# Routing the first chunks of a mixture-of-experts kernel earlier, and moving shared work and tables between its stages

## The reference

```python
scores = sigmoid(x @ gate_w.T)
choice = scores + gate_bias            # 8 groups of 8 experts
group_scores = sum(top_k(choice.reshape(T, 8, 8), 2)[0], -1)
# keep the 4 best groups, set the rest of choice to 0, take the 8 best experts
w = scores[chosen] / (sum(scores[chosen]) + 1e-20) * 2.5
out = sum over experts of w * down(silu(x @ gate.T) * (x @ up.T)) + shared(x)
```

## Time and profile before

| | |
|---|---|
| Runs shown | 659.68 us median of 3 (657.02 to 660.19) |
| The profiled execution | 659.67 us, of which the span of instructions is 657.9 us |
| Busy: PE, DVE, POOL, ACT | 588.1, 461.0, 444.8, 325.7 us |
| Granted TensorE clock, mean | 0.966 of full speed |

### The profile page before, as it was taken

The page is one execution under the profiler, slowest core; times in us unless marked ns, Lnnn a source line. Parts: engine busy times, 40 slices in busy tenths (PEclk is TensorE's granted clock), DMA queues, the critical chain, the costliest instruction groups (busy, mean ns, idle before and its releaser), DMA issues.

```text
span 657.9 us, 13016 instructions
## 1 busy us (share of the span) xinstructions
PE 588.1 (89%) x3456; PEld 472.5 (72%) x3457; DVE 461.0 (70%) x1311; ACT 325.7 (50%) x637; POOL 444.8 (68%) x464
## 2 busy tenths in 40 slices
PE   2986988888889899999996999999999999999980
PEld 2655666665655899999994999999995666666640
DVE  3446688888756789767773567677475598868785
ACT  8474866665553454555552455555552135252332
POOL 1003777777777777777776777777764777777773
PEclk9988899998997999999998999999999999999995
DMA  8962666661112678777755688888866223222122
GB/s 211 383 133 52 138 156 144 148 141 53 53 49 84 179 230 237 230 227 224 230 159 141 184 235 228 242 232 234 228 198 203 53 53 95 56 69 65 52 65 64
DMA packets 124609, 101.35 MB, mean 154 GB/s; under 512 B 15334, under 2 KB 114494, under 8 KB 124094
## 3 DMA queue, kind: packets, MB, share of 16 engines
q1 hardware_dynamic: 63766, 48.41, 27.9%
q0 software_dynamic: 14336, 29.39, 15.3%
q10 hardware_dynamic: 46464, 23.07, 12.1%
HBM read 52.58 MB, written 48.23 MB: 153 GB/s over the span
## 4 chain that ended last, share of the span: by engine, by line
PE 41%; POOL 31%; issue 12%; DVE 5%; DMA 4%; ACT 3%; SPq 1%; POOLq 0%; DVEq 0%; ACTq 0%
POOL xs_dram L513 29%; PE GU L820 8%; PE OT L840 6%; PE GU L880 4%; PE GU L881 4%; PE XT L889 4%; PE HT L829 3%; PE XT L809 3%; DMA arena<-os_dram,gslots 2%; POOL arena L518 2%; PE GU L601 1%; PE GU L752 1%; PE GU L751 1%; DMA xs_dram<-x1r,slots 1%; SPq L444 1%
## 5 line engine op out<-in xcount | busy, mean ns | idle before, releaser
L513 POOL DMA_INDIRECT xs_dram<-x1r,slots x224 | 225.7, 1007 | 123.5 <-issue 67.5
L518 POOL DMA_INDIRECT arena<-os_dram,gslots x224 | 217.0, 969 | 80.6 <-issue 64.8
L820 PE MATMUL GU<-wgu_sb,arena 128*128 x704 | 121.5, 316 | 0.1
L820 PEld LDWEIGHTS GU<-wgu_sb,arena 128*128 128x128 f32 x704 | 106.3, 192 | 1.2 <-issue 0.9
L1513 DVE TENSOR_TENSOR mlpw_sb<-GU,mlpw_sb 128x352 f32<-128x352 f32 x88 | 46.1, 524 | 73.6 <-ACT mlpw_sb L1084 70.0
L840 PE MATMUL OT<-wd_sb,arena 88*128 x704 | 93.7, 276 | 1.8 <-ACT ol L1094 1.7
L1094 ACT ACTIVATE ol<-OT 128x512 f32<-128x512 f32 x88 | 52.5, 597 | 80.7 <-PE OT L840 80.7
L840 PEld LDWEIGHTS OT<-wd_sb,arena 88*128 88x128 f32 x704 | 85.5, 192 | 3.0 <-issue 2.6
L1576 DVE SCALAR_TENSOR_TENSOR x_all<-arena,wk,x_all 128x128 f32<-128x128 f32 x224 | 66.3, 344 | 4.7 <-DMA arena<-os_dram,gslots 2.8
L1084 ACT ACTIVATE mlpw_sb<-GU 128x352 f32<-128x352 f32 x88 | 40.7, 463 | 49.3 <-PE GU L820 48.7
L1188 ACT ACTIVATE key<-GU 128x512 f32<-128x512 f32 x44 | 26.2, 596 | 69.9 <-PE GU L881 69.8
(11 more groups left out here) (206 smaller groups left out, 897.2 us busy)
## 6 DMA issues: line engine op xcount, KB each, us to landing
arena<-xs_dram SPq DMA_DIRECT2D x352, 64.0 KB
os_dram<-ol ACTq DMA_DIRECT2D x88, 256.0 KB
xs_dram<-ol SPq DMA_DIRECT2D x16, 512.0 KB
wgu_sb<-wgu_dram SPq DMA_DIRECT2D x1, 5632.0 KB
xs_dram<-x1r,slots POOLq DMA_INDIRECT x224
arena<-os_dram,gslots POOLq DMA_INDIRECT x224, 2.6
wd_sb<-wd_dram SPq DMA_DIRECT2D x1, 2816.0 KB
x_all<-x_dram SPq DMA_DIRECT2D x8, 256.0 KB, 5.7
```

The source lines that it names most:

```text
L513: g.indirect_dma_start(out=xs[b], out_offset=bass.IndirectOffsetOnAxis(ap=slots[:, t * K + k:t * K + k + 1], axis=0), in_=x1r[:, t, :], in ...
L518: return g.indirect_dma_start(out=gbuf[:, g_ % 2, t - SETS[g_][0], k, :], out_offset=None, in_=os[batch_of(t)], in_offset=bass.IndirectOff ...
L820: ins = mm(GU[:, 2 * r + i // 2, (i % 2) * 2 * I:(i % 2 + 1) * 2 * I], xg[:, r, i * P:(i + 1) * P], wgu_sb[:, bass.ds(at[i], 2 * I)], star ...
```

## The change

Chunks 0 and 1 are both routed whole within their own step (EARLY). Chunk 0's tile 0 goes through the choice by itself, with its own ranks, slots and semaphores, before the other three. The scores go straight into rw, and only chunk 7 multiplies them by the choice there; the mask becomes one predicated copy of zeros in place of a multiply and an add. The shared expert of chunk 2 moves ahead of batch 0 and those of chunks 3 and 4 between the batches; after batch 1 remain 5 to 7. The norm of chunk 7 moves behind ACT's silus of chunk 1. Ranks and tables of chunk 6 move into the first eight quads of batch 0, in the bank MI (rank_bank), as do batch 0's gather slots; slot_weights start nine quads later (W0).

```diff
-EARLY = 0
+EARLY = (0, 1)
+W0 = 9
-SH_A, SH_B = 2, 3
+SH_A, SH_B = 3, 5
-SUMS_IN_DENSE = {4: (2, 2, 8), 5: (10, 1, 8), 6: (26, 1, 8), 7: (38, 1, 5)}
+SUMS_IN_DENSE = {4: (3, 2, 8), 5: (15, 1, 8), 6: (30, 1, 8), 7: (40, 1, 2)}
...
@@ POOL, scatters @@
                 if t % CT == 0:
                     pool.wait_ge(s_x1r, t // CT + 1)
+                if t == 0:
+                    pool.wait_ge(s_slot_e, 1)
+                elif t == 1:
+                    pool.wait_ge(s_slot, 1)
+                elif t % CT == 0:
                     pool.wait_ge(s_slot, t // CT + 1)
...
@@ PE, step @@
-                if c == EARLY:
+                if c in EARLY:
                     logits(c)
                 if mlp:
                     mlp_block(k - 1, 1)
+                if c == 0:
+                    first_ranks()
...
-                if c == EARLY:
+                if c in EARLY:
                     for m in range(NM // 2):
                         mlp_down(k - 1, m)
+                    if c == 1:
+                        square_sums(k)
                     ranks(c)
                     for m in range(NM // 2, NM):
                         mlp_down(k - 1, m)
...
@@ PE, between front and batch 0 @@
-            shared_from(0, SH_A)
+            for c in range(SH_A):
+                shared_block(c, 0)
+                shared_block(c, 1)
+                if c:
+                    shared_down(c - 1)
+            pe.wait_ge(s_res, 1)
+            transpose_x1(NS, NC + 1)
+            shared_down(SH_A - 1)
+            logits(NS)
...
@@ PE, first_quads @@
+                n = UN if b else 2 * UN
+                for u in range(n):
+                    quad(b, Q0[b] + u, u % UN)
+                    if b == 0 and u == 1:
+                        ranks(NS - 1)
+                    if b == 0 and u == 3:
+                        starts(NBAT - 1)
+                    if b == 0 and u == 5:
+                        tile_experts(NBAT - 1)
...
@@ ACT, the front @@
-                if k - 2 == EARLY:
+                if k - 2 in EARLY:
                     nc.scalar.preload_act_table(ACT.Sigmoid)
                     take_x1(k - 2)
                     scores(k - 2)
...
@@ ACT, between front and batch 0 @@
-            root_v(NS)
-            norm_v(NS)
-            nc.scalar.preload_act_table(ACT.Silu)
             for c in range(SH_A):
                 for j in range(SJ):
                     shared_silu(c, j)
+                if c == SH_A - 2:
+                    nc.scalar.preload_act_table(ACT.Sqrt)
+                    root_v(NS)
+                    nc.scalar.preload_act_table(ACT.Silu)
+                    norm_v(NS)
+            take_x1(NS)
+            nc.scalar.preload_act_table(ACT.Sigmoid)
+            scores(NS)
+            nc.scalar.preload_act_table(ACT.Silu)
...
@@ DVE @@
+                then(v.tensor_scalar(m2[:, own], m1[:, own], GONE, None, ALU.not_equal))
+                then(v.copy_predicated(ch4[:, own, :], bc(m2[:, own].bitcast(U32).unsqueeze(2), P, n, EG),
+                                       bc(zero[:, 0:1].unsqueeze(2), P, n, EG)))
...
+            def take_first_ranks():
+                dve.wait_ge(p_rank_e, 1)
+                v.tensor_tensor(key[:, 0, :], HT[:, 0:E], sel[:, 0, :], ALU.mult).then_inc(s_key_e, 1)
+                dve.wait_ge(s_key_e, 1)
+                then(v.max(keys[:, 0, :], key[:, 0, :]))
+                v.tensor_scalar(slots[:, 0:K], keys[:, 0, :], float(P - 1), None, ALU.add).then_inc(s_slot_e, 1)
...
+                if front and c == 1:
+                    conv(k)
+                if c == 0:
+                    group_sums(c, 0, 1)
+                    group_seconds(0, 1)
+                    compare_groups(0, 1)
+                    mask_groups(0, 1)
+                    choose(c, 0, 1)
                 if mlp:
                     hidden(k - 1, 0)
                     hidden(k - 1, 1)
-                if c == EARLY:
+                if c == 0:
+                    take_first_ranks()
+                    group_sums(c, 1, CT)
...
+                    choose(c, 1, CT)
+                if c == 1:
+                    group_sums(c)
                     group_seconds()
                     compare_groups()
                     mask_groups()
                     choose(c)
+                if c in EARLY:
                     hidden(k - 1, 2)
                     hidden(k - 1, 3)
                     take_ranks(c)
...
@@ DVE, batch 0 @@
+                if q == 1:
+                    gather_slots(0, 0, half0)
                 if q == 2:
+                    take_ranks(NS - 1)
+                    count_tiles(NBAT - 1)
+                if q == 3:
+                    gather_slots(0, half0, TFIRST[1])
+                if q == 4:
+                    place_tiles(NBAT - 1)
...
+                if q == 6:
+                    weight_columns(NBAT - 1)
...
+                if q == 13:
                     choose(NS)
+                if q == 14:
+                    gather_slots(1, half1, NST)
...
+                if q % 2 and q >= W0:
+                    slot_weights((q - W0) // 2)
```

More of the change, by code:

```diff
@@ L723, in step @@
                         mlp_down(k - 1, m)
-                if front:
+                if front and c != 1:
                     square_sums(k)
-                if mlp and c != EARLY:
+                if mlp and c not in EARLY:
                     for m in range(NM):
@@ L1324, in group_seconds @@
-            def group_seconds():
-                then(v.tensor_tensor(tb4[:, :, 6:8], tb4[:, :, 2:4], tb4[:, :, 4:6], ALU.max))
-                v.tensor_tensor(pairs[:, :, 0:1], tb4[:, :, 0:1], tb4[:, :, 1:2], ALU.add)
-                then(v.tensor_tensor(pairs[:, :, 1:3], tb4[:, :, 0:2], tb4[:, :, 6:8], ALU.add))
-                then(v.tensor_reduce(gs, pairs, AX_X, ALU.max))
-            def compare_groups():
-                for i in range(CT):
+                n = slice(first * NG, end * NG)
@@ new lines, in group_sums @@
+                then(v.tensor_tensor(choice[:, first:end, :], rw[:, c * CT + first:c * CT + end, :],
+                                     bc(gbias_sb[:, :].unsqueeze(1), P, end - first, E), ALU.add))
+                lo, hi = ch4[:, n, 0:EG // 2], ch4[:, n, EG // 2:EG]
+                v.tensor_tensor(ta4[:, n, 0:4], lo, hi, ALU.max)
+                then(v.tensor_tensor(ta4[:, n, 4:8], lo, hi, ALU.min))
+                v.tensor_tensor(tb4[:, n, 0:2], ta4[:, n, 0:2], ta4[:, n, 2:4], ALU.max)
@@ L1333, in compare_groups @@
+            def compare_groups(first=0, end=CT):
+                for i in range(first, end):
                     ins = v.max(gtop[:, i, :], gs[:, i * NG:(i + 1) * NG])
                 then(ins)
-                then(v.memset(gtop[:, :, TOPG:NG], NOWHERE))
-                for i in range(CT):
+                then(v.memset(gtop[:, first:end, TOPG:NG], NOWHERE))
+                for i in range(first, end):
                     ins = v.match_replace(out=m1[:, i * NG:(i + 1) * NG], in_to_replace=gtop[:, i, :],
@@ L1362, in take_ranks @@
             def take_ranks(c):
+                first = 1 if c == 0 else 0
+                own = slice(c * CT + first, (c + 1) * CT)
                 dve.wait_ge(p_rank, c + 1)
-                v.tensor_tensor(flat(key[:, span(c), :]), HT[:, 0:CT * E], flat(sel[:, ring(c), :]),
+                v.tensor_tensor(flat(key[:, own, :]), rank_bank(c)[:, first * E:CT * E], flat(sel[:, ring(c), :])[:, first * E:],
                                 ALU.mult).then_inc(s_key, 1)
                 dve.wait_ge(s_key, c + 1)
-                for t in tiles(c):
+                for t in tiles(c)[first:]:
@@ L1469, in _ @@
                     norm2(k)
[L1470 removed]
+                if route and c not in EARLY and c < ROUTED:
                     compare_groups()
@@ L1623, in plain @@
                             quad(b, i * UN + u, u)
[L1625 to L1630 removed]
             def adding(b, g):
                 for k in range(K):
[L1635 removed]
+                    q = SUM_AT[g] + k
+                    quad(b, q, q)
+                    if q % 2 and q < 2 * NST + W0:
+                        slot_weights((q - W0) // 2)
```

240 lines of the change are left out of this document (118 added, 122 removed).

## The result

The changed kernel took 670.27 us (median of four executions, 668.02 to 675.64) beside 658.82 for the kernel before (657.02 to 660.19): a ratio of 1.0187, 95% interval 1.0119 to 1.0255. It is slower, as forecast, but by 11.5 us and not by 6.0. The profiled execution was the longest of the four, 675.64 with a span of 673.9; so its trace overstates the change by some five microseconds, and the first of the experiments takes a second trace of the same kernel.

A forecast was written before the change was run, and what follows sets the result against it. PE was taken to bound the kernel: its end of batch 1 plus a fixed tail of 162.5 us. Terms 4.0 - 3.3 + 4.5 + 0.8 = +6.0 gave 665.7 us; range 656 to 671.

The forecast's parts named there:

- front's end: Steps before batch 0: splitting chunk 0 and routing chunk 1 in step 3 make the front end 4.0 us late (1 to 7).
- front's end to batch 0: Stretch before batch 0: ranks and tables out, a shared chunk in, idle time and clock regained; 3.3 us earlier (1.5 to 5).
- batch 0: Within batch 0: moved routing 3.4 and DVE's bump 1.9, less load waits 0.8; 4.5 us later.
- between the batches: Between batches: second shared chunk +5.2, idle -3.1, slow clock -1.3; +0.8 us (-1 to +2).
- batch 1 and tail: Batch 1 to the end: fewer shared chunks there change nothing, as POOL's 112 gathers end the kernel; 0 (-1.5 to +1).
- the half clock as a rival: Step 3, products after PE's two stands: the clock falls there; chance 0.13.
- the split's price: Step 2: routing chunk 0's first tile alone issues DVE's small operations twice, delaying the front by 1.1 us (0.5 to 2).
- Chunk 1's slots: Step 3: chunk 1's slots come at 90.2, ahead of 93.7, when POOL wants them.
- POOL's long wait before the first gather: Before batch 0's first gather: POOL waits over ten microseconds, not 3; a sign that the forecast is right.
- the bump: Batch 0, quad 13: a choice and a slot_weights together, 4.40 us on DVE, delay PE by 1.9 us (0 to 4).
- The rival of POOL: Hand-over of batch 0: PE finishes before the last scatter, so earlier scatters carry through both gather streams; 652.8 us, chance 0.12.
- one fixed tail: After batch 1 on PE: the kernel's end is PE's end of batch 1 plus a fixed 162.5 us.

The follow-up runs named there:

- e11: The changed kernel with filler matmuls that fit PE's waits in steps 2 and 3, one or two products of 512 columns each: 665.44 us, ratio 1.0097.
- e5: The changed kernel with four shared chunks behind batch 1 and one between the batches, instead of three and two: 664.35 us, ratio 1.0082.
- e3: The changed kernel with chunk 0 routed whole, its first tile not by itself; chunk 1 still within step 3: 666.57 us, ratio 1.0119.
- e4: The changed kernel with chunk 1 routed a step later, as before; chunk 0's first tile still by itself: 669.42 us, ratio 1.0161.
- e8: The changed kernel with the choice of the last chunk's experts moved from quad 13 to quad 16: 666.55 us, ratio 1.0107.
- e9: The changed kernel with the shared chunks where the kernel before had them: two ahead of batch 0, one between the batches, five behind: 663.71 us, ratio 1.0071.
- e6: The changed kernel with no shared chunk between the batches and five behind batch 1: 664.79 us, ratio 1.0088.
- e2: The changed kernel with the front of before: chunk 0 whole and chunk 1 routed a step later: 666.38 us, ratio 1.0110.
- e10: e9 with the choice of the last chunk's experts at quad 16 instead of 13: 662.90 us, ratio 1.0061.
- e7: The changed kernel with a longer filler of 12 matmuls of 512 columns in PE's waits of steps 2 and 3: 670.37 us, ratio 1.0170.
- e12: The kernel before with the filler of e11 at its places in step 2 only: 658.92 us, ratio 0.9988.

## Why the prediction was wrong

The direction and the place were right, and the size was off: +8.7 to +11.5 instead of +6.0. Each term, with the first trace and the second:

| term of the sum | forecast | first trace | second trace |
|---|---|---|---|
| front's end | +4.0 | +8.2 | +3.6 |
| front's end to batch 0 | -3.3 | -3.6 | -3.6 |
| batch 0 | +4.5 | +5.5 | +4.0 |
| between the batches | +0.8 | +5.9 | +2.7 |
| batch 1 and tail | 0 | +0.0 | +0.4 |
| sum (spans 657.9; 673.9; 664.9) | +6.0 | +16.0 | +7.0 |

**The clock is the step that failed.** The prediction had the row for it (logits of 1.64 after 1.25 of idle; the granted clock over them is 0.62) and kept it out of the sum, with the half clock as a rival of 0.13 in step 3 alone. The new order puts that wait in step 3 as well, ahead of a chain (logits, scores, products, routing) with nothing to cover it; in the first trace steps 2 and 3 ended 2.6 us later than forecast (95.31 for 92.7), steps 4 to 7 lost 1.7 more (103.30 for 101.61 in the second trace), and e11 puts the usual loss in steps 2 and 3 at 2.2 to 2.5. So the sum had the clock at nothing there, and the runs showed 2.2 to 2.5 for steps 2 and 3 in a usual execution: more in the first trace, and nothing beyond the forecast in the second, whose front ends at 193.99. How it divides between the two steps is not shown; the kernel before, which has the waits of step 2 too, gained 0.7 at most from the same filler there. The rival had the right place and too low a chance. What it costs shows in the two traces: in step 3 of the first the logits and the three pairs behind them take 1.91, 2.02, 1.92 and 1.92 (granted clock 0.50 to 0.56), in the second 1.10, 1.08, 1.02 and 1.10, 3.5 less, but there PE stands 1.58 among them, so they end 1.6 sooner after the start of the logits. What no single trace showed is that it comes and goes: the kernel's executions reach from 666.64 to 675.64, those of the kernel before, in the result's four, from 657.02 to 660.19 (to 662.11 over all the runs).

**Between the batches** the term was mis-sized by 1.9. The step was "the load's wait and the clock's fall go": it took all 3.1 of the idle time away. In the second trace PE idles 13.86 - 12.29 = 1.57 there. Two waits of 0.78 (the rows at 375.64 and 377.07) are the chain from a shared product to its sum on DVE, to the next transposes, to their copy on ACT; there is no load in them, and another chunk does not fill them. In the kernel before the idle time was three waits:

```profile
355.94 2.34 PE L771 MATMUL XT<-sd_sb,arena 88*128 88x128 f32 x16 [1.41 <-DVE arena L1481]
...
359.06 1.12 PE L809 MATMUL XT<-ident,arena 128*128 128x128 f32 x4 [0.78 <-DVE x_all L1487]
```

and the 0.93 for a load at 361.11. The second chunk fills the wait of 1.41, the 0.78 stays, and behind the 0.93 for the load stood a 0.78 for ACT's copy, so an early load gains 0.15 there (in e5, with one chunk and early loads, the three waits are 1.41, 0.79 and 0.78). The clock came back in the second trace (1.00 instead of 0.84), but was worth some 0.85 and not 1.3: the two pieces of work above take 2.34 and 1.12 us at a granted 0.84 and 0.50, and 1.95 and 0.66 in the second trace. The front, the stretch behind it and batch 0 lie 1.2 under their forecasts in the second trace and hide part of the 1.9; that is luck.

**Right, and shown.** The first scatter (51.28 and 51.55; forecast 51.6) and the split's price (1.0 to 1.4 in e3; 1.1, where the prediction's own terms, 13.1 - 11.9, give 1.2). Chunk 1's slots: 89.77 in the second trace, forecast 90.2, and no stop of POOL; e4 shows the stop that would have come. The stretch ahead of batch 0 (-3.6; -3.3): its idle time falls from 24.04 - 19.20 = 4.84 to 2.49, by 2.35 for the 1.6 of the sum, and its clock rises from 0.86 to 1.00, where PE is busy for 17.91, which is 3.05 less than 19.20 - 3.44 + 5.2, for the 3.4 of the sum. POOL's long wait before the first gather (17 to 22; "over ten"). Batch 0: PE's busy time rises by 135.88 - 131.89 = 4.0 (the moved routing was put at 3.4), the bump is 1.5 (1.9 without a working; the prediction's own 4.40 less the 3.0 of a quad is 1.4; e8), and the load waits that go are 1.5 (0.8). SP's loads start 14.0 after the front's end in both traces of the changed kernel (the forecast had 13), so the early scatters did not bring them forward.

**Right in kind only.** "Ten microseconds of shared work are pulled ahead of the point that sets the end": undoing this gives 4.2 (e9), one chunk of it 3.6 (e5). But the premise of one fixed tail fell in e6: when PE is early enough, the gathers of batch 0 set the end. The rival of POOL had the wrong place: not the hand-over of the scatters, which have 17 us to spare, but the hand-over from the gathers of batch 0 to those of batch 1.

**Not settled.** The time that the front's delay costs at the end (1.5 by e2, inside the intervals); how much of the 2.0 us by which e9's median stands further above the kernel before than its trace is the gathers' stream, as in e10's trace; and why that stream takes 150 us in one trace and 152.6 in another.

## What to carry to other kernels

Starting an engine earlier pays only if it is late at the hand-over where its work is wanted; here its waits of 3 and 5 us said that it was not, and the price fell on the engine that was. Before work is moved ahead of the point that sets the end, see which bound lies just behind that point: here the gathers' own stream, 150 us and more from its first. And an order that makes PE stand in an uncovered chain has to be priced with the half clock (here 2.2 to 2.5 us), in several executions and not in one. Filler that fitted the wait took that loss back here (e11, 665.44 us for 667.93), and filler that was longer than the wait cost more than it brought (e7, 670.37); in the kernel before, filler brought nothing that could be told.

## What the runs showed of the hardware that was not expected

The same eight products after the same wait of 1.25 us took 1.10 us in one execution of a program, at a granted clock of 1.00, and 1.91 in another, at 0.52; one program's eight executions spread over 9 us (1.3%) with nothing changed, and with some 7 us of filler matmuls (e11: three of 1.02, one of 1.88, one of 1.96) five executions lay within 0.6. That is not a rule: the kernel before with such filler spread over 4.1 in twelve (e12, 656.73 to 660.87). Filler begun at half clock took longer (6.41 at a granted clock of 0.57, against 3.60 at 1.00 for the same eight passes in step 3 of e7); the clock was back behind it (1.00 from 70.65 to 75), at a price of four microseconds more than PE's wait of 2.46.

From the last down to the gather that its store releases it was 5.0 to 6.4 us for batch 0 (354.48 to 359.43 in e5, 350.98 to 357.34 in e2), but about 10 for batch 1 (495.39 to 505.25 in the kernel before), where SP loads the dense weights at the same time (issued at 496.62 and 504.25). That this load is the cause was not tried. In the traces of e3 and e8 it was 12.1 and 12.6: there the last of the sixteen parts of the last store landed 2.1 and 2.7 behind the other fifteen (at 512.78 and 511.25).
